# Decoder layer on one core: roots of variances moved from GpSimd to ScalarE, loads placed later, two PSUM places and two TensorE steps exchanged

## The reference, cut to what matters

```python
x = x + local_attention(layernorm(x))                  # 16 heads of 8, causal
x = x + cross_attention(layernorm(x), ctx, times, bucket_ids)
y0 = layernorm(x)                                      # (x - mean) / sqrt(var + 1e-5)
y1 = ln(y0 + mha(y0), g1, b1)                          # 4 heads of 32, across the batches
x = x + ln(y1 + moe(y1), g2, b2)                       # 8 experts, capacity 256 each
```

## Time and profile before

| | |
|---|---|
| Median of 3 runs | 389.6 us (388.9 to 390.59) |
| The profiled execution | 389.38 us, its span 387.6 us |
| PE busy | 338.2 us, 87% of the span |
| DVE busy | 271.8 us, 70% |
| ACT busy | 148.1 us, 38% |
| POOL busy | 100.5 us, 26% |
| DMA moved | 28.63 MB, 74 GB/s over the span |

### The profile page before, as it was taken

One profiled execution on the slowest core, in us unless ns is written; L12 is line 12 of the kernel. 1 busy time (PEld: TensorE's weight loads), 2 busy tenths in 40 slices (PEclk: granted clock), 3 DMA queues, 4 the chain that ended last, 5 costly groups with the idle time before them and its releaser, 6 DMA issues.

```text
span 387.6 us, 12234 instructions
## 1 busy us (share of the span) xinstructions
PE 338.2 (87%) x4813; PEld 227.2 (59%) x4813; DVE 271.8 (70%) x703; ACT 148.1 (38%) x398; POOL 100.5 (26%) x165
## 2 busy tenths in 40 slices
PE   3798898999999899999999998876899599699994
PEld 2444454666665464655555555663656346599993
DVE  5775787666667788878898986343455189448996
ACT  2123364556665354554546463432244412100000
POOL 1136443000011435453233423126000023301111
PEclk9999999999999999999999999996999999569999
DMA  8999533344722525125000000000000000000001
GB/s 223 339 244 299 133 90 107 118 131 140 215 88 96 128 76 138 49 84 111 2 3 3 2 2 3 3 0 3 2 2 3 2 0 1 2 2 13 22 23 54
DMA packets 29192, 28.63 MB, mean 74 GB/s; under 512 B 4312, under 2 KB 24808, under 8 KB 29008
## 3 DMA queue, kind: packets, MB, share of 16 engines
q1 hardware_dynamic: 26848, 24.24, 22.1%
q0 software_dynamic: 1280, 3.15, 3.1%
q10 hardware_dynamic: 1008, 0.46, 0.5%
HBM read 20.17 MB, written 7.67 MB: 72 GB/s over the span
## 4 chain that ended last, share of the span: by engine, by line
PE 73%; ACT 9%; DVE 6%; issue 5%; another core or an unknown queue 3%; DMA 2%; ACTq 1%; POOL 1%; POOLq 0%; DVEq 0%
PE ps L1067 9%; PE ps L1084 8%; PE ps L1029 7%; PE ps L1370 7%; PE ps L1039 3%; PE ps L1003 3%; PE ps L1114 3%; PE ps L1148 3%; PE ps L982 3%; ACT pT L804 3%; PE ps L995 2%; PE ps L1219 2%; ACT pT L920 2%; PE ps L1161 2%
## 5 line engine op out<-in xcount | busy, mean ns | idle before, releaser
L804 ACT ACTIVATE pT<-ps 128x512 f32<-128x512 f32 x128 | 70.4, 609 | 98.1 <-PE ps L1039 88.3
L407 DVE TENSOR_REDUCE m_pad<-ps 128x8 f32<-128x1024 f32 x32 | 39.2, 1224 | 35.0 <-PE ps L1067 35.0
L701 POOL TENSOR_TENSOR rstd<-veps,minus_half 128x1 f32<-128x1 f32 x32 | 19.1, 598 | 137.7 <-DVE veps L372 137.0
L383 DVE TENSOR_TENSOR p_sb<-qk_sb,heads 128x512 f32<-128x512 f32 x64 | 44.0, 687 | 1.8 <-DMA ident_bf<-c_ident_bf 1.4
L410 DVE TENSOR_REDUCE m_pad<-ps 128x8 f32<-128x1024 f32 x32 | 38.9, 1215 | 0.0
L1067 PE MATMUL ps<-p_sb,qk_sb 32*128 32x512 f32 x256 | 38.4, 671 | 0.0
L1084 PE MATMUL ps<-pT,p_sb 128*32 128x128 f32 x1024 | 36.8, 276 | 1.5 <-issue 1.5
L1029 PE MATMUL ps<-p_sb,qk_sb 32*128 32x512 f32 x256 | 38.0, 655 | 0.0
L765 POOL TENSOR_TENSOR rs<-ve,half 128x2 f32<-128x2 f32 x16 | 11.2, 698 | 99.2 <-DVE ve L610 99.2
L1039 PE MATMUL ps<-mT,negsel 32*128 32x128 f32 x512 | 34.6, 364 | 0.8 <-issue 0.7
L1370 PE MATMUL ps<-mexp,pT 128*128 128x128 f32 x256 | 34.4, 291 | 0.6 <-DVE pT L675 0.6
(11 more groups left out here) (176 smaller groups left out, 640.3 us busy)
## 6 DMA issues: line engine op xcount, KB each, us to landing
room<-mask_rows SPq DMA_DIRECT2D x32, 128.0 KB, 3.3
wkv_sb<-wkv SPq DMA_DIRECT2D x23, 128.0 KB
kv_sorted<-room SPq DMA_DIRECT2D x5, 512.0 KB, 4.8
ctx_sorted<-room SPq DMA_DIRECT2D x1, 1472.0 KB, 12.5
tk<-fside SPq DMA_DIRECT2D x1, 1024.0 KB, 9.5
mask_rows<-y1T SPq DMA_DIRECT2D x8, 128.0 KB, 2.7
out<-y SPq DMA_DIRECT2D x8, 128.0 KB, 1.8
x_sb<-x SPq DMA_DIRECT2D x1, 768.0 KB, 6.9
```

The source lines that it names most:

```text
L383: return dve.tensor_tensor(dst, rows.unsqueeze(1).broadcast_to([128, QUADS, S]), heads[:, 0, :].unsqueeze(2).broadcast_to([128, QUADS, S]) ...
L407: dve.tensor_reduce(m4[:, 0:2, 0:QUADS], ps[:, 0:2, :].rearrange("p g (j k) -> p g j k", j=QUADS), AX.X, ALU.max).then_inc(s["max_low"], 1)
L701: pool.tensor_tensor(rstd[:, :], veps[:, :], minus_half[:, :], ALU.pow)\
L804: act.activation(pT[:, t % 2, g, :, :], quad[4 + g], ACT.Exp).then_inc(s["exped"], 1)
```

## The change

Four things:

1. The power -0.5 leaves POOL. ACT computes it as exp(-0.5 ln(var + 1e-5)), two small instructions: `norm_root`, `y0_root` and `pair_roots`. The DVE instruction that added 1e-5 goes, since Ln takes it as a bias column. In periods below 0 `norm_root(p+4)` is the first call of ACT's period; from 0 on it stands between the last exponential and `copy_qk`, and `y0_root(p-21)` behind it.
2. The transpose of normed rows goes to bank 0, columns 128 to 255, was bank 1; its copy on ACT moves between the first and the second exponential. The output projection goes to bank 5, columns 384 to 511, was bank 2, and PE runs `project_qkv(p+3)` ahead of `project_out(p-3)`. `turn_heads` no longer waits for the residual of the step before, only for its copy.
3. SP issues `bucket_weights(0)` and `(1)` right behind the context. The times go out once `pv_done` is 2, the cross weights with the first sorted store, the expert weights in 8 pieces from step 15 on, the small weights between them. The DVE masks begin in period 4, was 3.
4. With the powers gone, nothing on POOL stands between the 16 scatters.

The diff, cut to its core:

```diff
 sync
+            sp.wait_ge(s["pv_done"], 2)
+            times_and_pads()
...
+                if i == 0:
+                    cross_weights()
...
+            sp.wait_ge(kv_in[0], 32)
             masks_by_group(1)
+            expert_weights(0)
+            expert_weights(1)
             masks_to_rows(2)
+            small_weights(0)
             masks_by_group(2)
...
+            def expert_weights(e):
+                sp.wait_ge(s["pv_done"], 15 + e)
+                sp.dma_start(w1t_sb[:, e, :, :], w1t[e].rearrange("(c p) d -> p c d", p=128))\
+                  .then_inc(s["experts_in"], 16)
+                sp.dma_start(w2_sb[:, e, :, :], w2[e].rearrange("(c p) d -> p c d", p=128))\
+                  .then_inc(s["experts_in"], 16)
 vector
-            def norm_variance(t):
-                dve.wait_ge(s["bn_step"], 2 * t + 2)
-                if t >= 1:
-                    dve.wait_ge(s["pow_done"], t)
-                dve.tensor_scalar(veps[:, :], mv[:, 1:2], EPS, None, ALU.add).then_inc(s["veps_ready"], 1)
 gpsimd
-                pool.tensor_tensor(rstd[:, :], veps[:, :], minus_half[:, :], ALU.pow)\
-                    .then_inc(s["pow_done"], 1)
 scalar
+            def norm_root(t):
+                if t == 0:
+                    act.wait_ge(s["ones_ready"], 1)
+                act.wait_ge(s["bn_step"], 2 * t + 2)
+                act.activation(lnvar[:, :], mv[:, 1:2], ACT.Ln, bias=eps_col[:, :]).then_inc(s["ln_step"], 1)
+                act.wait_ge(s["ln_step"], t + 1)
+                if t >= 1:
+                    act.wait_ge(s["xn_ready"], t)
+                act.activation(rstd[:, :], lnvar[:, :], ACT.Exp, scale=-0.5).then_inc(s["root_done"], 1)
...
             for p in PERIODS:
+                if p < 0 and live(p + 4):
+                    norm_root(p + 4)
                 if live(p):
                     exp_group(p, 0)
+                if live(p + 3) and p != -1:
+                    turn_xn(p + 3)
+                if live(p):
                     exp_group(p, 1)
...
-                if live(p + 3) and p != -1:
-                    turn_xn(p + 3)
...
                     exp_group(p, 3)
+                if p >= 0 and live(p + 4):
+                    norm_root(p + 4)
+                if 0 <= p - Y0_STATS - 1 < B:
+                    y0_root(p - Y0_STATS - 1)
                 if live(p + 3) and p != -1:
                     copy_qk(p + 3)
 tensor
-                pe.matmul(bank[2][:, 128:256], ofT[:, :], w_out_sb[:, t // B, :], start=True, stop=True)\
+                pe.wait_ge(s["exped"], min(4 * t + 14, 4 * T))
+                if t >= 1:
+                    pe.wait_ge(s["resid_done"], t)
+                pe.matmul(bank[5][:, 384:512], ofT[:, :], w_out_sb[:, t // B, :], start=True, stop=True)\
...
+                if live(p + 3) and p != -1:
+                    project_qkv(p + 3)
                 if live(p - 3):
                     project_out(p - 3)
-                if live(p + 3) and p != -1:
-                    project_qkv(p + 3)
```

More of the change, by code:

```diff
@@ L428, in residual @@
                 rows = x_sb[:, t % B, :]
-                dve.tensor_tensor(rows, rows, bank[2][:, 128:256], ALU.add).then_inc(s["resid_done"], 1)
+                dve.tensor_tensor(rows, rows, bank[5][:, 384:512], ALU.add).then_inc(s["resid_done"], 1)
             def bucket_hots():
@@ L759, in _ @@
                     pool.tensor_tensor(y0[:, b, :], y0[:, b, :], ob_rows[:, :], ALU.add).then_inc(s["y0_biased"], 1)
-            def powers(k):
-                for i in range(B // 2):
-                    pool.wait_ge(s["ve_ready"], B + k * (B // 2) + i + 1)
-                    pool.tensor_tensor(rs16[:, 2 * i:2 * i + 2], ve16[:, 2 * i:2 * i + 2], half16[:, 0:2], ALU.pow)\
-                        .then_inc(s["rs_ready"], 1)
-            powers(0)
             pool.wait_ge(s["crep_copied"], 1)
@@ L774, in _ @@
                                    .then_inc(s["cblk_ready"], 1)
-            powers(1)
         @block.scalar
@@ L780, in turn_xn @@
                 act.wait_ge(s["xT_done"], t + 1)
-                if t >= 4:
-                    act.wait_ge(s["pv_done"], t - 3)
                 if t >= 1:
                     act.wait_ge(s["qkv_done"], t)
-                act.copy(xnT[:, :], bank[6 if t == 2 else 1][:, 256:384]).then_inc(s["xnT_copied"], 1)
+                act.copy(xnT[:, :], bank[6 if t == 2 else 0][:, 128:256]).then_inc(s["xnT_copied"], 1)
             def turn_max(t):
@@ L813, in copy_qk @@
                 act.wait_ge(s["qkv_done"], t + 1)
+                if t >= 6:
+                    act.wait_ge(s["resid_done"], t - 5)
                 if t >= 4:
@@ L940, in _ @@
             mha_sums(3)
+            pair_roots(0, 0)
             for b in range(B):
+                if b % 2 == 0 and b + 2 < B:
+                    pair_roots(0, b // 2 + 1)
                 act.wait_ge(s["y1T_done"], b + 1)
@@ L956, in _ @@
             act.copy(keptT[:, :], bank[4][:, 0:128]).then_inc(s["keptT_copied"], 1)
+            for i in range(B // 2):
+                pair_roots(1, i)
         @block.tensor
@@ L972, in turn_xn @@
                     pe.wait_ge(s["xnT_copied"], t)
-                pe.transpose(bank[6 if t == 2 else 1][:, 256:384], xn[:, :], ident[:, :]).then_inc(s["xT_done"], 1)
+                pe.transpose(bank[6 if t == 2 else 0][:, 128:256], xn[:, :], ident[:, :]).then_inc(s["xT_done"], 1)
             def turn_o(t):
```

144 lines of the change are left out of this document (71 added, 73 removed).

## The result

The change made the kernel slower: 410.13 us (median of 4 runs, 408.6 to 412.28) against 390.1 us for before (388.9 to 390.98), a ratio of 1.052, 95% interval 1.046 to 1.058. I had forecast 382.0, and 389.5 as the upper end. Later runs added a second fact that has to be known from the start: on five later occasions, when before took about 382 us, the same change (run on two of them) took 1.001 of it, and on one more occasion it took 1.052 of it again. On that one the 13 runs of before lay between 385.3 and 395.05 us, and the ratio is formed with the five that count as fast, whose median is 387.33. I call the two conditions **quiet** and **held**.

What follows compares the result with a forecast made beforehand. PE (87% busy) was taken as the bound, with ofT's latency on its path. From 389.4 us, +4.9 for the fill and -4.6, -4.6, -1.1, -1.3, -0.8 elsewhere summed to -7.5: 382 us, range 375.5 to 389.5.

Steps and rivals of the forecast that it cites:

- POOL's queue loses waits only, so the scatters end earlier: POOL's DMA queue in the loop: counted as free; the load of sorted rows that waits for the scatters also ends earlier.
- rival B: Early part gains nothing: back-to-back scatters cause the stalls, PE's rate rises 2 us later; 386.5 to 387; chance 0.21 shared.
- Periods 0 to 5, -4.6: First six periods: 2.3 us from PE's new order plus 2.3 of stalls given back (bounds 0 and 5).
- the exchanged order: PE in each loop period: projections run while ofT is copied, hiding its latency; 0.44 less a period, 0.38 with local steps.
- Periods 12 to 20, -4.6: 0.38 us saved in 12, 0.45 in each of 13 to 20, and 0.6 for a PE stall beside the first gather.
- The fill, +4.9: Before period 0: roots in ACT's in-order list delay copies, PE and the first maxima; costs 4.9 us, bounds 2.0 and 7.
- A root, 0.46: Two one-column ACT activations in place of POOL's power: Ln 0.27 plus Exp 0.19 us, bounds 0.15 each and 0.6.
- from period 22: Late loop, where y0's root also delays `copy_qk`: gain 0.25 in 21 and 22, 0.1 in each of 23 to 28, 1.1 us.
- Rival C: ACT sets the pace, `copy_qk` behind the roots: 397 us at 0.9 a root, deciding from about 0.7; chance 0.11.
- Sorted periods, 0: Periods 6 to 11: PE waits at L1148 for the exponentials, so time it saves ahead is waited there; gain 0.
- End of the loop, -1.3: A 0.43 us wait for a residual goes, and a 0.87 us wait for a power becomes a root; 1.3 us saved.
- Layernorms, -0.8: Behind the loop: no DVE add on 8 pairs saves 0.4 us; a root replacing add and power at the end saves 0.4.

Runs made afterwards that it cites:

- paced: The change with scatters waiting for ACT's roots, fill and y0 roots, `cblk` and small weights moved, pair roots ahead; 392.92 us held, 1.0135 of before.

## Why the prediction was wrong

**The step that failed most** stands among the things costed at nothing: "POOL's queue loses waits only, so the scatters end earlier". It loses waits, and they had been the gaps between groups of indirect DMAs. In the held condition the signals of PE get through late while such DMAs go out. Period 0 with the 16 in a row took 16.6 us more than in before (23.39 against 6.78; 22.67 and 6.89 on the second held occasion, unpaced and paced), and the gathers, which now start beside the by-key products and not 1.5 us ahead, put the exponentials of 13 to 19 off by 1.5 to 2.1. Of the 27 us that the hold cost the change in the first measurement (410 against 383), before paid 8 (390 against 382). I had written this mechanism down as rival B ("the scatters, now back to back, cause the stalls") and priced it by the excess that before showed, 2.3 us. That excess was the price of groups of three; a run of 16 cost seven times as much. The bound from above should have come from a row: ACT stood 4.9 us beside one group, and there are five groups, so 25 as an estimate. Without the hold the change would have been called the same as before (1.001), and the forecast, 7.5 us less than before, would have been wrong as well, by the terms that follow.

**Periods 0 to 5, -4.6.** Wrong in both conditions: +11.9 held, +0.2 quiet. In the quiet one there were no stalls to remove: before's 45.4 was 38.0. Nor did the exchanged order give its 0.38 a period there: they took 38.6 us with the order undone and 38.2 in the change, 0.06 a period.

**Periods 12 to 20, -4.6.** Held +3.4, quiet -5.2. The exchanged order was right as a mechanism; its size is 0.31 a period by the run without it, 0.45 was forecast. Of the quiet gain 3.5 us is one period in which before had stood 9.64.

**The fill, +4.9.** Right in mechanism and size: +5.4, copy of step 1's turned rows at 12.72 (said 11.7), maxima at 21.11 (20.5), first products at 27.64 (27). In the quiet pair of profiles it was +6.9, at the bound, but the first products of one kernel come up to 1.1 us apart from profile to profile (27.03 to 28.16 for the change). **A root, 0.46:** 0.52. The mechanism of ACT's list was right, and from period 22 it was mis-sized: I let one root move the copies by 0.35, it was 0.46, PE waited 0.58 for `y0T_copy`, and the periods took 6.6 in place of 6.35: +0.6 held and +0.8 quiet, not -1.1. Rival C's threshold wasn't reached. **Sorted periods, 0:** right. **End of the loop, -1.3:** -1.5, right. **Layernorms, -0.8:** wrong, +3.1 held and +2.5 quiet, since a 1.4 us wait for a root behind copies of ACT's list pushed the last rows under `cblk`.

What stays open: what the hold is. Shown are its conditions (POOL issuing indirect DMAs, some occasions) and its marks (late updates by PE, PE's torn mask tiles, SP's slow issues). No run in the held condition paced the gathers, or the scatters alone. SP's loads aren't needed for it beside gathers: from 154 to 161 us in the first trace next to nothing but the gathers moved (32 GB/s), and the exponential was late. Whether they are needed for the 23 us of period 0 no held run tells.

## What to carry to other kernels

A slow helper instruction between DMA issues may be what spaces them: before removing it, list what runs back to back once it is gone, and price the longest run, not the mean gap. An instruction put into an in-order engine delays everything behind it by its full wait, so place it where that engine already stands idle; three such moves (fill, y0, the product behind the rows) turned 1.00 into 0.98 in the quiet condition. And when experiments find none of the effect, run the unaltered kernels beside them before explaining anything.

## What the runs showed of the hardware that I had not expected

- On some occasions PE's semaphore updates come late while POOL issues indirect DMAs, and whatever waits for them starts late: 1.5 us for a pair, 4.7 us at the first exponential beside sixteen, 16 us on that period. In periods 14 to 19 of the first trace the exponential came 1.61 to 1.69 us after the start of the pair's second. Updates by ACT, DVE and POOL stayed on time. On other occasions the same program showed 0.02. The Trainium skill ("SBUF — State Buffer", SBUF: two separate sides) says that DMA can't slow a compute instruction. The traces agree, held ones too: an exponential took 613 ns in the held trace of the change and 608 in the quiet one; what came late was its start.
- PE stops of 1.5 to 2.4 us lie at a fixed place in stretches of 256 of its records, with bulk loads beside, as if it ran dry of instructions. The Trainium skill ("Runtime: NRT & Kernel Launch", Instruction fetch mechanics) calls the cost of crossing such a boundary mostly hidden. In the loop it was, except for these.
- A DVE instruction with two SBUF inputs waited out a 3.7 us POOL product, its own work being 0.35 us.
